# Layer 1's attention begins in another order: maxima between key pieces, first keys of three groups copied

## What is computed

```
x = x + _L0_xattn_ref(_layernorm(x, axis=-1), ctx_1024, ctx_1024, ...)
x = x + _L0_ffn_ref(_layernorm(x, axis=-1), ...)
x = x + _L1_xattn_ref(_layernorm(x, axis=-1), ctx_1024, ctx_1024, L1_xattn_Wq, L1_xattn_bq,
                      L1_xattn_Wk, L1_xattn_bk, L1_xattn_Wv, L1_xattn_bv, L1_xattn_Wo, L1_xattn_bo)
x = x + _L1_ffn_ref(_layernorm(x, axis=-1), ...)
...
```

## Time and profile before

| | us |
|---|---|
| median of three runs | 4126.5 |
| lowest and highest | 4123.52, 4128.83 |
| the profiled execution | 4126.28 |
| its span, first to last instruction | 4124.4 |

### The profile page before, as it was taken

The page is one execution under the profiler, slowest core; times in us unless marked ns, Lnnn a source line. Parts: engine busy times, 40 slices in busy tenths (PEclk is TensorE's granted clock), DMA queues, the critical chain, the costliest instruction groups (busy, mean ns, idle before and its releaser), DMA issues. The chain is left out here.

```text
span 4124.4 us, 71234 instructions
## 1 busy us (share of the span) xinstructions
PE 3840.4 (93%) x26117; PEld 2765.1 (67%) x26117; DVE 2632.9 (64%) x6105; ACT 2668.3 (65%) x4648; POOL 951.4 (23%) x842
## 2 busy tenths in 40 slices
PE   7898899999889999999999999978999999998885
PEld 6654444445467777777777777745888888886455
DVE  7655888888565666566566566556566666654762
ACT  6523577777447676767677676734777777776752
POOL 2100000000000000000000000001777777876434
PEclk9999999999899999999999999988999999999997
DMA  2100433322100000000000000010000000000003
GB/s 79 40 1 27 75 52 51 49 42 26 47 13 1 13 1 13 1 13 13 1 13 1 13 1 1 1 45 17 9 9 9 9 9 1 1 1 14 28 5 105
DMA packets 61039, 87.82 MB, mean 21 GB/s; under 512 B 13177, under 2 KB 51467, under 8 KB 59501
## 3 DMA queue, kind: packets, MB, share of 16 engines
q1 hardware_dynamic: 54729, 73.68, 8.1%
q10 hardware_dynamic: 4464, 6.30, 0.4%
q0 software_dynamic: 1504, 3.28, 0.2%
HBM read 58.07 MB, written 10.08 MB: 17 GB/s over the span
## 5 line engine op out<-in xcount | busy, mean ns | idle before, releaser
L2366 POOL TENSOR_TENSOR L3a_p_lo<-L3a_wq,L3a_p_hi 128x512 fp32r<-128x512 f32 (+1 forms) x480 | 627.9, 1325 | 207.5 <-ACT L3a_p_hi L2303 196.1
L1226 DVE CUSTOM_DVE_ANT_0 L2a_sc<-L2a_score,L2a_mask_n 128x804 f32<-128x804 f32 x512 | 500.0, 991 | 211.7 <-issue 195.1
L1116 ACT ACTIVATE L2a_pt<-L2a_ring 128x512 f32<-128x512 f32 x768 | 424.7, 597 | 138.6 <-PE L2a_ring L1005 133.6
L604 ACT ACTIVATE L1a_work<-L1a_ring 128x1024 f32<-128x1024 f32 x416 | 410.7, 1028 | 148.5 <-PE L1a_ring L436 147.9
L720 DVE TENSOR_REDUCE L1a_mx<-L1a_ring 128x2 f32<-128x1024 f32 x384 | 454.4, 1221 | 37.4 <-PE L1a_ring L455 31.9
L2458 DVE TENSOR_REDUCE L3a_mx<-L3a_ring 128x1 f32<-128x402 f32 (+2 forms) x640 | 322.7, 539 | 197.4 <-PE L3a_ring L2155 188.6
L1101 ACT ACTIVATE L2a_sc<-L2a_sc,L2a_nb 128x1608 f32<-128x1608 f32 x256 | 418.4, 1636 | 34.0 <-DVE L2a_nb L1231 34.0
L1005 PE MATMUL L2a_ring<-L2a_ident,L2a_sc 128*128 128x128 f32 x3072 | 425.0, 278 | 15.6 <-ACT L2a_sc L1101 9.2
L1005 PEld LDWEIGHTS L2a_ring<-L2a_ident,L2a_sc 128*128 128x128 f32 x3072 | 342.4, 141 | 86.1 <-issue 35.9
L2302 ACT ACTIVATE L3a_wq<-L3a_ring 128x512 f32<-128x512 f32 (+1 forms) x480 | 285.1, 594 | 160.0 <-PE L3a_ring L2077 114.3
L1020 PE MATMUL L2a_res<-L2a_pt,L2a_v 128*64 128x256 f32 (+1 forms) x3328 | 373.4, 381 | 1.4 <-ACT L2a_pt L1116 1.4
(11 more groups left out here) (742 smaller groups left out, 8180.9 us busy)
## 6 DMA issues: line engine op xcount, KB each, us to landing
L1a_keys<-L1a_k_hi SPq DMA_DIRECT2D x224, 52.0 KB
L1a_kt<-in_ctx_t SPq DMA_DIRECT2D x8, 800.5 KB, 4.4
L2a_ct<-in_ctx_t SPq DMA_DIRECT2D x8, 800.5 KB, 4.3
L1a_keys<-L1a_k_lo SPq DMA_DIRECT2D x112, 52.0 KB
L0a_cx<-in_ctx SPq DMA_DIRECT2D x16, 320.0 KB, 4.0
L3a_cx<-in_ctx SPq DMA_DIRECT2D x16, 320.0 KB, 3.7
L2a_mask_u<-in_mask SPq DMA_DIRECT2D x16, 200.1 KB, 4.4
L3f_sent<-in_L3f_blank SPq DMA_DIRECT2D x1, 3128.0 KB
```

The source lines that it names most:

```text
L604: act.activation(probs[:, (par * NU + u) % c.PS, :, :], ring[tile][:, :, :], ACT.Exp).then_inc(tile_free[tile], 1)
L1116: ins = act.activation(pt[:, t:t + 4, g // 3, q], bank[:, :].rearrange("p (t q) -> p t q", t=4), ACT.Copy)
L1226: dve.tensor_tensor_reduce(sc[:, two, e, w].rearrange("p (k j) -> p k j", k=2), score[e][:, :, 0:CH], mask_n[:, r % 2, w].rearrange("p (k ...
L2366: pool.tensor_tensor(p_lo[0:r, at % PL, 0:W], probs[0:r, at % 2, 0:W], p_hi[0:r, at % PH, 0:W].bitcast(F32), ALU.subtract).then_inc(part_o ...
```

## The change

For batch 0, group 0's keys and queries are still computed with replicated weights, but first and with only that group's weights loaded (`wkr` shrinks from four groups to one). Groups 1 to 3 no longer have their 12 key pieces computed this way. Instead the parts k_hi and k_lo are computed once for batch 0 (steps `late0` to `late3`) and copied: SP makes the copies for r = 0, 1, POOL's queue those for r = 2, 3, 18 each. Four further DMAs on SP copy the constant rows to groups 1 to 3.

A new string LEAD gives the order of the opening. Group 0's tops pieces (T) stand between key pieces, the other groups' queries (`own1` to `own3`), the turns of the tokens of batches 2 to 7 (`late4` to `late6`), the four query pieces (`late7` to `late10`) and the bias (`late11`). All `late` steps use the one bank `res`, and each waits for the one before. x is normalized on DVE for the first four tiles and on POOL for the other twelve; the reciprocal root moves from fourteen small DVE instructions to one POOL power; the clearing of tile `v` moves from DVE to POOL. Loads are split in two sets. Bodies from the first scores on keep their order.

```
+    LEAD = "late0 T0 own1 T3 late1 T6 own2 T9 late2 T1 own3 T4 late3 T7 value0 T10 T2 value1 T5 late4 T8 T11 late5 T12 T13 late6 H value2 late7 W value3 late8 U0 late9 U1 U2 late10 U3 late11 U4"
...
             held.clear_old(sp)
             load_context(1)
-            sp.wait_ge(ql_ok, QC)
+            sp.wait_ge(keys_ok, KB)
+            for r in range(4):
+                at = slice(32 * r + 3 * c.DH, 32 * r + 32)
+                sp.dma_start(keys[at, 0, 1:NG, :].bitcast(F32),
+                             keys[at, 0, 0:1, :].bitcast(F32).broadcast_to([c.DH, NG - 1, JP])).then_inc(same_in, 16)
+            sp.wait_ge(late_free, LK)
+            replicate_keys(0, range(1, NG), range(2))
+            sp.wait_ge(late_free, LQ)
             for copy, rows in enumerate((q_hi, q_hi, q_lo)):
                 sp.dma_start(scr_q[:, copy].rearrange("r d g j -> r (d g) j"), rows.bitcast(F32)).then_inc(q_put, 16)
             sp.wait_ge(q_put, 48)
             sp.wait_ge(blank_ok, 1)
+            sp.wait_ge(same_in, 64)
...
+                elif b == 0 and n in c.opening:
+                    pe.wait_ge(queries_ok, g + 1)
+                    pe.wait_ge(same_in, 64)
+                    pe.wait_ge(k_in[g], 96)
+                    pe.wait_ge(k_also[g], 96)
...
+            def late(b, par, k):
+                if b:
+                    return
+                if k:
+                    pe.wait_ge(late_free, k)
+                if k < LK:
+                    w = span_of(k)
+                    pe.matmul(res[:, 0:w.stop - w.start], wk[:, :], kt[:, 0, w], start=True, stop=True).then_inc(late_full, 1)
...
+                elif k < LQ:
+                    n = k - LX
+                    if n == 0:
+                        pe.wait_ge(more_ok, 1)
+                    pe.matmul(res[:, :], wq[:, :], yt[:, n * 512:(n + 1) * 512], start=True, stop=True).then_inc(late_full, 1)
...
-                if k == 0 and not (isinstance(b, int) and b == 1):
-                    for g in range(NG):
-                        act.wait_ge(k_in[g], b * 192 - 192)
+                if k == 0:
+                    for g in range(0 if b > 1 else 1, NG):
+                        act.wait_ge(k_in[g], (b - 1) * 192 + (96 if g else 0))
+                        if g and b == 1:
+                            act.wait_ge(k_also[g], 96)
...
+            pool.memset(v[:, :, :, :], 0.0)
+            pool.wait_ge(mv_ok, 1)
+            rsqrt_chunk(pool, st, half, slice(0, NT)).then_inc(rs_ok, 1)
...
+            pool.wait_ge(late_free, LK)
+            for g in range(1, NG):
+                for r in range(2, 4):
+                    for copy, rows in enumerate((k_hi, k_lo, k_hi)):
+                        at, of = 32 * r + copy * c.DH, 32 * r + g * c.DH
+                        pool.dma_start(keys[at:at + c.DH, 0, g, :].bitcast(F32), rows[of:of + c.DH, :].bitcast(F32)).then_inc(k_also[g], 16)
```

More of the change, by code:

```diff
@@ L66, in __init__ @@
         self.nc = nc
-        self.old, self.now, self.later = [(ExitStack(), []) for _ in range(3)]
+        self.old, self.now, self.later, self.kept = [(ExitStack(), []) for _ in range(4)]
     def next_phase(self):
@@ L85, in finish @@
     def finish(self):
-        for s in self.now[1]:
+        for s in self.now[1] + self.kept[1]:
             self.nc.sync.sem_clear(s)
@@ L168, in turn, with run_bodies @@
         return at % tiles, at // tiles
-def run_bodies(eng, order, steps):
+def run_bodies(eng, order, steps, lead=None):
     def body(b, par, offs):
-        for kind, off, n in order:
+        for kind, off, n in lead if lead and b == -1 else order:
             if off in offs and kind in steps:
@@ L307, in build_heads @@
         piece = lambda i: (i // 6, i // 3 % 2, i % 3) if i < 12 else (i - 12, None, 3)
[L308 to L312, removed]
+        first = {("key", 0): 2, ("turn_x", 0): 0, ("key", 1): 3, ("own", 0): 1, ("key", 2): 4, ("key", 3): 5,
+                 ("own", 1): 6, ("own", 2): 6, ("own", 3): 6}
+        first_at = lambda kind, n: list(first).index((kind, n))
+        first_bank = lambda kind, n: aux[:, :] if first[kind, n] == 6 else bank_of(first[kind, n])
+        cleared = lambda banks, k: max([i + 1 for i, bank in enumerate(list(first.values())[:k]) if bank in banks], default=0)
+        LK, LX = KB, KB + QC - 1
+        LQ = LX + QC
         block = done.enter_context(nc.Block())
@@ L536, in finish @@
                 mm.then_inc(aux_full, 1)
-            run_bodies(pe, c.order, dict(scores=scores, tops=tops, values=values, key=key, value=value,
-                                         rows=rows, denominator=denominator, spread=spread, project=project, finish=finish))
+            run_bodies(pe, c.order, dict(scores=scores, tops=tops, values=values, key=key, value=value, own=own, late=late,
+                                         rows=rows, denominator=denominator, spread=spread, project=project, finish=finish), c.lead)
         @block.scalar
@@ L759, in finish @@
                 dve.nop().then_inc(xo_ok, 1)
-            run_bodies(dve, c.order, dict(tops=tops, shift=shift, rows=rows, key=key, denominator=denominator, spread=spread,
-                                          finish=finish))
+            run_bodies(dve, c.order, dict(tops=tops, shift=shift, rows=rows, key=key, own=own, late=late, denominator=denominator,
+                                          spread=spread, finish=finish), c.lead)
 class MaskedPlan:
```

284 lines of the change are left out of this document (175 added, 109 removed).

## The result

The changed kernel takes 4133.3 us (median of 11 runs, 4128.8 to 4140.6) against 4124.8 us for the kernel before (11 runs, 4122.2 to 4129.2): a ratio of 1.0021 with a 95% interval of 1.0013 to 1.0029. It is slower by 8.5 us, where 0.2% is 8.25 us: the interval reaches to both sides of what was called no change (5.4 to 12.0 us). The forecast was 4130, 3.3 us less. The profiled execution took 4134.2 us, its span 4132.1.

A forecast was written before the change was run, and what follows sets the result against it. SP's chain from the query writes to the last key copy was taken as the bound. Start +4.4, queue +1.0, slack -1.6 gave +3.8 us on the profiled 4126.28, then 0.2 for the median: 4130.3 us, range 4120 to 4142.

The forecast's parts named there:

- The chain and its 1:1 rule: SP's queue, query writes to last key copy: 99.3 us, unchanged; the phase's end moves with its start, beyond 1.6 us slack.
- Both waits: Waits for copies: PE 15 us before batch 1's first tops, ACT 6 us at batch 2's first key step.
- Rival A: First scores 18 us sooner carry through the body, giving 4108.5 us; chance 0.10.
- (a): Head of the phase: statistics, norm, turns and first key pieces bring DVE to the first k_lo at about 388 us.
- (b): DVE's work from first k_lo to fourth q_lo: 27.4 us, so query writes start at 415.4 without idling.
- (c): Idling in the query pieces' round trips through bank `res`: query writes start at 422.0, 4.4 us later than before.
- (d): Key copies on SP's and POOL's queues ahead of the query writes: landed by 421.5; delay taken as 1.0 us.
- the sum: Query writes' start +4.4, queue +1.0, slack -1.6: +3.8 us on the time.
- The two restart terms of 1.5 us: After the waits: PE running ahead while ACT waits, -1.5 us, and PE's half clock after a stall, +1.5 us.
- Rival B: The two copy queues share engines: fully, 4140.5 us; lower half, only half of POOL's copies share, 4132; chance 0.28.
- signs named for B: Copies landing above 1.2 us apart while both queues run; wait for query writes ending over 34.3 us after issue.
- Rival C: No DVE idling before the fourth q_lo: writes at 415.4, 4122.6 us; its chance lies within the forecast's 0.60.

The follow-up runs named there:

- the cut: Changed kernel with each of the three query writes cut into four of 32 rows: 4112.7 us, -12.2 us against the kernel before.
- all three edits: Changed kernel with query writes cut, constant rows' copies on GpSimd's queue, and GpSimd's copies of groups 2 and 3 held until group 1 landed: 4108.6 us.
- the version where group 1 landed in time: Changed kernel with GpSimd's twelve copies of groups 2 and 3 held until all twelve of group 1 had landed: 4134.6 us.

## Why the prediction was right, and where it was not

**The chain and its 1:1 rule: right.** 98.9 us against 99.3 forecast, and late writes in the otherwise untouched kernel moved the chunk by the delay less 1.6 us. Both waits came where they were forecast, 13.7 us (15) and 3.8 us (6). The second is short because PE took 29.1 us from batch 1's first maxima to the chunk where 26.7 were reckoned. The 12.9 us by which the first scores start sooner brought nothing, and Rival A did not occur. With a shorter chain its price is nearly borne out, at 18 us for scores 18 us sooner: with the cut the scores come 13.6 us sooner and the time falls by 12.2, and with all three edits 19.5 and 17.1.

**(a) and (b): right.** The first k_lo was forecast 17.3 us from the mark and started at 17.7, and k_lo was complete at 29.2 (29.6). The shift ended at 37.4, where 39.3 had been forecast.

**(c), the fourth q_lo: right by itself, wrong in the kernel as it was.** Forecast 51.3 us from the mark. It came at 56.4, and at 50.2 in the version where group 1 landed in time. There it was partly luck: two errors offset each other, the shift 2 us sooner and round trips of 2.9 to 4.4 us in place of 2.6 to 3.0.

**(d) is the step that failed.** "Group 1's twelve have landed at 409.5", 38.8 us from the mark, was over 9 us early: PE could not begin on them before 48.5. The eighteen copies of SP were to end by 417 and ended at 426.6. GpSimd's eighteen issues were put at 17.7 us, from the row of an indirect DMA, and took 9.6 (401.29 to 410.85), so its copies of groups 2 and 3 were on the engines while group 1's were still under way. And the queue's delay of 1.0 us, taken as small because the two queues might add up, stood for two holds that the second queue caused. Writes 9.6 us later in place of 5.4 is 4.2 of the 4.7 us by which the chunk's shift (8.5) exceeds the sum (+3.8). The other 0.5 is the chunk's start 4.2 us behind the last copy's issue, where 3.3 had been reckoned, less a chain shorter by 0.4. The two restart terms of 1.5 us cancelled in the sum, and no run measures either; the shift is 8.5 us at batch 2's chunk and 7.1 at batch 7's.

**The time itself came out closer than the mechanism.** The forecast of 4130 stood on a kernel before of 4126.5, whose median is now 4124.8. That is why the time misses by 3.3 us where the difference misses by 4.7.

**Rival B, lower half: in its size this is what took place.** "If only half of them do, 27 x 0.92 = 24.8, at 425.1", worth 4132. The copies took 25.6 us and ended at 426.6, the time is 4133.3. That the time fits so well is partly luck, for B had SP's own copies hold the writes, and in the changed kernel the last q_lo held them 1.7 us longer. The full case, 33.1 us, writes at 433.4 and 4140.5, is what the kernel with all copies on one queue showed: 32.7 us, 433.4 and 4142.3. Of the signs named for B the first was there (1.42 us a copy, above 1.2). The second, 34.6 us from the writes' issue to their end where 34.3 was the mark, is too small to count: the untouched kernel with late writes also shows 34.3, and GpSimd's last copy had landed by 420 us, before the writes began. The rows could not decide between adding and sharing, and my 1.0 us took adding. The page "DMA: Bandwidth & Descriptors" of the Trainium skill, section "Why a DMA increments its semaphore by 16 and not by 1", gave the half whose size took place, with SP's copies on the lowest-numbered engines and half of GpSimd's among them; which engines carried which packets no row here shows. The Trainium skill's page "Trainium Kernel Development and Optimization", section "Key Constraints", says that a second issuing engine saves issue time only. Here it did more: 78 to 83 GB/s with two queues and 58 with one, 1.4 times as much.

**Rival C, no idling:** did not occur; DVE idled for 3.2, 5.5 and 1.5 us between the first q_lo and the third, 10.2 us of the 13.5 there.

## What to carry to other kernels

Find the chain that ends last and ask from which event it is counted; work that starts sooner elsewhere brings nothing until that event or the chain moves, and then the two edits are worth more together (-12 us) than their sum (+9). A transfer off the critical path still takes engines from one that is on it: give the copies that are waited for first the queues to themselves, and put a buffer's overwriting step on the list of deadlines, not its readers only. Look first at how many engines a DMA on the chain uses; here 19 us lay in an outer dimension of 4.

## What the chip showed that I had not expected

GpSimd's direct copy of 8 rows costs 0.52 to 0.56 us of issue, the first one 0.81 (the eighteen run from 401.29 to 410.85 us), against 0.91 us a copy on SP alone. Its queue then moves 0.49 MB in the first 10 us, and SP's beside it 0.28. In this window it also has 402 packets for 0.49 MB, where SP's queue alone had 160 for 0.57 MB. 364 of the 480 in the window are under 512 B, against 75 of 161. Why its copies are cut finer, and whether that is what slows SP's, no run here tells.

A DMA's issue on SP is no fixed cost: the same copy took 0.62 to 7.4 us (the longest right behind the uncut query writes), and four loads 6.8 or 15.3 us (the longer beside GpSimd's copies of the constant rows).
